# PE's opening fillers as 84 small matmuls in column tiles, and VectorE's order around slab 0's split

## The reference

```python
def _cin_layer(x0, x, kernel):
    m = x0.shape[1]
    h_prev = x.shape[1]
    W = kernel.reshape(m, h_prev, kernel.shape[1])
    return jnp.einsum('bmd,bhd,mho->bod', x0, x, W)
x = x0
finals = []
for k in (k1, k2, k3):
    x = _cin_layer(x0, x, k)
    finals.append(jnp.sum(x, axis=-1))
logit = jnp.concatenate(finals, axis=-1) @ kf
```

## Time and profile before

| | |
|---|---|
| median of 3 runs | 305.47 us (304.95 to 306.73) |
| the profiled execution's own time | 306.67 us |
| its span | 304.7 us |
| busy: PE, DVE, ACT, POOL | 97%, 64%, 79%, 75% of the span |
| chain that ended last | PE 94%, of it L558 74% of the span |
| mean granted PE clock | 0.988 of full |

### The profile page before, as it was taken

One profiled execution on the slowest core, in us unless ns is written; L12 is line 12 of the kernel. 1 busy time (PEld: TensorE's weight loads), 2 busy tenths in 40 slices (PEclk: granted clock), 3 DMA queues, 4 the chain that ended last, 5 costly groups with the idle time before them and its releaser, 6 DMA issues.

```text
span 304.7 us, 7927 instructions
## 1 busy us (share of the span) xinstructions
PE 295.1 (97%) x3189; PEld 87.0 (29%) x3189; DVE 195.1 (64%) x211; ACT 241.6 (79%) x232; POOL 228.3 (75%) x132
## 2 busy tenths in 40 slices
PE   7769999999999999999999999999999999999996
PEld 2442222222322222222222222232222222222221
DVE  1635857657777666667766666677766666777632
ACT  1564997979979797988979797997979798897921
POOL 7456967878798687878788687879868787878800
PEclk9968999999999999999999999999999999999999
DMA  7999999594876849486784838487683839500000
GB/s 244 405 412 421 389 407 407 186 352 203 319 307 247 347 148 345 169 344 258 304 315 189 357 142 353 198 318 301 254 342 148 360 150 346 224 0 2 2 0 1
DMA packets 15414, 77.84 MB, mean 255 GB/s; under 512 B 1832, under 2 KB 2088, under 8 KB 7720
## 3 DMA queue, kind: packets, MB, share of 16 engines
q1 hardware_dynamic: 15256, 77.49, 64.9%
q10 hardware_dynamic: 144, 0.15, 0.3%
HBM read 77.63 MB, written 0.01 MB: 255 GB/s over the span
## 4 chain that ended last, share of the span: by engine, by line
PE 94%; DMA 2%; issue 1%; DVE 1%; ACT 1%; SPq 0%; DVEq 0%
PE acc L558 74%; PE acc L566 10%; PE rot L544 8%; DMA xc<-x_chunks 2%; PE acc L590 1%; PE acc L577 1%; ACT prod L198 1%; PE acc L637 0%; SPq L236 0%; DVE xy L492 0%; DVE sums L495 0%; DVE low L456 0%; ACT split L303 0%; PE acc L631 0%; PE acc L614 0%
## 5 line engine op out<-in xcount | busy, mean ns | idle before, releaser
L558 PE MATMUL acc<-prod,w 128*32 128x512 f32 x2048 | 229.1, 598 | 0.2 <-issue 0.2
L389 POOL TENSOR_TENSOR prod<-u,v 128x1024 f32<-128x1024 f32 x64 | 152.9, 2390 | 14.9 <-PE acc L558 11.1
L558 PEld LDWEIGHTS acc<-prod,w 128*32 128x32 f32 x2048 | 64.1, 110 | 147.7 <-issue 133.7
L283 ACT ACTIVATE prod<-rot 128x1024 f32<-128x1024 f32 x64 | 65.3, 1021 | 25.4 <-PE rot L544 24.9
L485 DVE TENSOR_TENSOR prod<-rot,u 128x1024 f32<-128x1024 f32 x64 | 77.7, 1214 | 4.8 <-PE rot L544 4.8
L492 DVE SCALAR_TENSOR_TENSOR xy<-acc,kzs,xsb 128x512 f32<-128x512 f32 x32 | 24.0, 751 | 85.8 <-ACT xsb L312 80.0
L485 DVE TENSOR_TENSOR prod<-rot,v 128x1024 f32<-128x1024 f32 x64 | 77.6, 1213 | 0.0
L399 POOL TENSOR_TENSOR split<-low,split 128x512 bf16<-128x512 f32 x31 | 36.1, 1165 | 32.1 <-ACT split L307 32.1
L291 ACT COPY feat<-u 32x2048 f32<-32x2048 f32 x31 | 58.9, 1899 | 0.6
L287 ACT ACTIVATE feat<-u 96x2048 f32<-96x2048 f32 x31 | 58.8, 1898 | 0.0
L395 POOL TENSOR_TENSOR low<-xc,split 128x512 f32<-128x512 f32 x31 | 36.2, 1167 | 10.1 <-ACT split L303 9.9
(11 more groups left out here) (44 smaller groups left out, 29.6 us busy)
## 6 DMA issues: line engine op xcount, KB each, us to landing
u<-u_rows SPq DMA_DIRECT2D x30, 1024.0 KB, 4.8
v<-v_rows SPq DMA_DIRECT2D x30, 1024.0 KB, 6.9
xc<-x_chunks SPq DMA_DIRECT2D x32, 256.0 KB, 6.9
u<-u_rows SPq DMA_DIRECT2D x4, 512.0 KB, 9.7
v<-v_rows SPq DMA_DIRECT2D x4, 512.0 KB, 11.7
u<-k3p SPq DMA_DIRECT2D x2, 512.0 KB, 5.3
v<-k2t SPq DMA_DIRECT2D x1, 512.0 KB, 6.7
fixs<-fixes SPq DMA_DIRECT2D x1, 256.0 KB, 7.6
```

The costliest lines, as they stand in the source:

```text
L283: nc.scalar.activation(prod[p][:, WW, pair(n)], rot[:, pair(n)], ACT.Square).then_inc(squares_ready, 1)
L389: nc.gpsimd.tensor_tensor(prod[p][:, UV, pair(half)], us[n][:, pair(half)], vs[n][:, pair(half)], ALU.mult).then_inc(uv_ready, 2)
L558: mm = nc.tensor.matmul(acc[p][h][quad(c), :], w[:, t, h * G:(h + 1) * G], prod[p][:, t, chunk(c)], start=(t == first), stop=(first is Non ...
```

## The change

PE's ten opening fillers of 128 x 512 become 21 rounds of four matmuls of 256 columns, each on one column tile of 32 (32 x 256 out), 84 in all. On DVE the copies of vt and v, with their waits, come ahead of the first subtraction of slab 0; before, they stood between the two.

```diff
-            split_low(0)
             dve.wait_ge(vt_ready, 1)
             nc.vector.tensor_copy(vts[:], vt_ps).then_inc(vts_ready, 1)
             dve.wait_ge(v_done, 1)
             nc.vector.tensor_copy(vk[:, 0:WRAP], v_ps).then_inc(v_ready, 1)
+            split_low(0)
             split_last(0)
...
+            def keep_clock_up_in_tiles(bank, count):
+
+
+                for _ in range(count):
+                    for c in range(CHUNKS):
+                        nc.tensor.matmul(bank[quad(c), 0:CHUNK // 2], idle[:, 0:M], idle[:, 0:CHUNK // 2], start=True,
+                                         stop=True, skip_group_check=True)
+
             pe.wait_ge(idle_ready, 1)
-            keep_clock_up(acc[1][0], 10)
+            keep_clock_up_in_tiles(acc[1][0], 21)
             pe.wait_ge(kz_in, 16)
```

## The result

| | before | changed |
|---|---|---|
| median, same chip, 8 runs each | 305.21 us (303.35 to 306.73) | 302.47 us (302.14 to 302.84) |
| ratio, 95% interval | | 0.9907 (0.9879 to 0.9935) |
| the profiled execution's own time | 306.67 us | 302.38 us |
| its span | 304.7 us | 300.6 us |
| mean granted PE clock of it | 0.988 | 1.00 |

The change makes the kernel 0.9% faster, 2.7 us by the medians. The forecast was 4.1. The two profiled executions do lie 4.1 us apart in span and 4.3 in their own time: the profile of before happened to be one of its slowest executions. That is the main thing to explain.

The account below looks back on a forecast made before the run. PE, busy 97%, bounds the kernel, so its slabs' start sets the end. Earlier copies, no hole and a kept clock, less what loads and ACT give back, leave 4.1 us: 305.47 - 4.1 = 301.4, range 300.4 to 304.6.

Parts of the forecast that it names:

- Fillers: PE's opening: 84 tile matmuls stream four side by side, end at 4.8 inside the wait for k3, price 0.
- rival D: Opening fillers: tile matmuls don't stream side by side, end at 19.1; +7.3, 312.8 us; chance 0.05.
- Copies: DVE's copies of vt and v ahead of slab 0's subtraction: L590 starts at 12.15, 0.95 us gained.
- Code: PE's instruction fetch: 148 more instructions get the packet requested earlier, so the 1.83 us hole in L590 goes.
- Rival C: L590: the hole stays as long, only 0.95 and some of the clock's cost gained; 303.9 us; chance 0.20.
- Clock: PE after L590: granted clock stays up, L577 costs 1.0 not 1.93, slab 0's contraction starts at 16.35, not 19.90.
- Rival B: PE from 17.5 to 24.4: the clock falls all the same; 2.9 ahead, 302.6 us; chance 0.20.
- Given back: Later slabs: loads, then ACT's lateness, bound; the lead shrinks from 5.3 at slab 1's rotation to 4.1 at slab 4's.
- The last step of the sum: Whole kernel: the 4.1 gain of the profiled execution subtracted from the median, 305.47 - 4.1 = 301.4.
- A: The main forecast for the whole kernel: 301.4 us, own range 300.4 to 302.5, chance 0.50.

Follow-up runs that it names:

- e2: The changed kernel with DVE's copies back in their old order, so the 84 fillers alone: 302.46 us, ratio 0.9905.
- e3: The kernel before with its ten whole fillers and only DVE's new copy order: 305.36 us, ratio 0.9991.
- e5: The changed kernel with 14 filler rounds of 384 columns in place of 21 of 256, 56 matmuls: 305.17 us, ratio 0.9977.
- e4: The changed kernel with seven whole fillers and 77 of 8 columns, 84 in all: 302.49 us, ratio 0.9914.
- e7: The changed kernel with all 84 fillers cut to 8 columns: 302.81 us, ratio 0.9926.
- e6: The changed kernel with ACT squaring slab 2's fields before the middle split of slab 3: 301.55 us, ratio 0.9885.
- e9: The same version as e6, run once more on another chip: 301.75 us, ratio 0.9894.
- e1: The kernel before once more, no edit, twelve executions: 304.14 us.

## Why the prediction was right or wrong

**Fillers: right.** They end at 5.77, covered. The forecast of 4.8 took the rate to rise at 3.9 as in the profile of before. In this execution they took 4.58 us, near the 4.5 of all 21 groups at the low rate, which I had as the other bound (5.7). Four column tiles stream side by side, in bf16 too; rival D needed an end after 11.8.

**Copies: right in size, wrong in worth.** L645 at 9.17 for 9.0, L590 at 12.25 for 12.15, the new wait of the rotation 0.33 for 0.4. But e2 loses none of it when it is taken out: behind it come loads that bound anyway. In e3 it is 1.1 us at the level 0.994 and 0.4 at 0.988, and the mix of levels hides it in the median.

**Code: right.** The packet came at 10.2 (forecast 9 to 10.5), the hole went, and no other came at the boundary in slab 0. e5 put the hole where the count says; e4 and e7 show that the number of instructions decides, and not what they stream. The place of the boundary was somewhat too early, as e5's longer hole shows. Rival C falls.

What makes the packet timely is where the waits lie. Before, PE goes from the boundary in L637 (some 10.6, by the count) to the end of its code at 14.8 in 4.2 us, less than the 6 that the code behind it takes to come (until 16.66). Now the stretch begins in the first L632, near 6, and has the waits for vts, the split and the tables in it, so that its end is reached at about 12.6 (an estimate: nine matmuls into L590), with the packet at 10.2 and its code some 2.4 later. That is hardly any slack.

The Trainium skill's rule (Runtime: NRT & Kernel Launch, Instruction fetch mechanics) of blocks of 256 instructions fits these runs; that a crossing is mostly hidden holds for the boundaries later in the kernel, where no idle of PE for "issue" over 0.3 us stands in the trace of before, and not for the one in L590, with 1.57 to 2.04 us in four profiles.

**Clock: right for the profile.** It stayed up, with 2.06 us of PE work in the stretch 14.1 to 17.5 where 2.4 were forecast. Rival B falls for nearly every execution: one of eight of the changed kernel was at 0.994, and cost 0.4 (302.84). That the hole brings the fall shows in the counts: with a hole in L590 (before, e3, e5) 76 of 84 executions were below the full clock, without one (the changed kernel, e2, e4, e6 to e9) 5 of 44.

**Given back: nearly right in sum.** 20.56, 26.16, 35.47 and 46.14 for 20.5, 26.1, 35.6 and 46.2. Within that, one wait was missed: after L590 PE waited 0.89 for L577 (0.43 before), as the timeline of ACT shows:

```profile
14.39 0.63 ACT L303 ACTIVATE split<-xc 128x512 bf16<-128x512 f32 x1 [1.22 <-DMA xc<-x_chunks]
14.93 0.25 ACT L326 COPY w<-acc 128x128 f32<-128x128 f32 x1
```

The copy of w stands in ACT's queue behind the split of slab 1, which waited for slab 1's x. It made the contraction 0.45 late (16.80 for 16.35), and the loads hid it again.

**The last step of the sum failed.** "The median of the runs shown is 1.2 lower than that execution, so against it: 305.47 - 4.1 = 301.4." The 4.1 was the gain of an execution with the long fall of the clock, 3.1 us of it (306.31 against 303.26). An execution of before without a fall has only 0.8 to gain, one with the short fall 2.5 (305.00 - 302.47). The clock's term had to be weighed by how often the fall comes: with 8, 32 and 21 of 61 executions the mean gain is (8 x 0.8 + 32 x 2.5 + 21 x 3.8) / 61 = 2.7, which is what was measured. (The shares of the levels move with the occasion; without e1's twelve the same sum gives 2.9.) A sign was there: three runs of before spread over 1.8 us, and I subtracted the same term from each.

That 302.47 still lies just inside A's own range (300.4 to 302.5) is partly luck: the high end was set by a rest of the hole and by new waits, and of these only the waits came. The median by itself, nearest to rival B's 302.6, would not have told A from B; the windows did.

What the hole and the chain cost by themselves is small for the same reason that the forecast gave for the whole: with the clock up, 2.0 us at slab 1 are 0.9 at slab 4.

## What to carry to other kernels

A hole on an engine that no semaphore ends, with a packet on the instruction queue ahead of it, is late code: count instructions back to the boundary before, and put cheap instructions into a wait that is there anyway. They cost nothing there and move the boundary ahead of other waits, so that the packet has these to come in. More instructions move every later boundary too, so each has to be placed again. Before a gain is subtracted from a median, see whether the profiled execution is a usual one: when runs of one kernel differ in granted clock, each level has its own gain. And when an engine starts earlier, the next thing to read is the queue of each engine that feeds it: here one instruction of ACT that waited ahead of work that was ready cost as much as the change had brought at full clock (0.9 and 0.8 us).

## What the hardware showed that was not expected

The clock falls in some executions of a program and not in others: with a hole of 1.57 us PE kept 2.4 GHz (e1's profile), with one of 1.83 us it lost it for 6.8 us. This is the window of e1 ahead of that point (PE 1.40 us of 3.40), and the one in the earlier trace rows had 1.17:

```profile
14.10:17.50 3.40, 1.40 (x61) 1.24 (x55) 0.73 (x1) 1.02 (x3) 1.37 (x2) 1.00 1.01 404
```

What decides between the three levels was not tried. The length of the hole is a candidate that four profiles can't settle: the clock fell behind 1.81, 1.83 and 2.04 us and not behind 1.57. That six of e1's twelve kept the clock and two of the other 49 speaks against chance in each execution alone.

A late packet's delay was much the same wherever it stood: from its start to PE's next record 2.4 us in before (14.2 to 16.66), 2.5 in e1 (13.9 to 16.41), 2.3 in e3 (13.3 to 15.68), 2.4 in e5 (12.8 to 15.16).
